# Layer one of a four-layer graph network: the destination's one-hot columns formed by ScalarE in two passes, for the next step, in place of VectorE's comparison

## The reference, cut to what matters

```python
src, dst = (edge_index[0], edge_index[1])
x = jnp.concatenate([node_features[src], node_features[dst], edge_features], axis=-1)
h = jax.nn.relu(x @ W1.T + b1)
messages = h @ W2.T + b2
agg = jax.ops.segment_sum(messages, dst, num_segments=node_features.shape[0])
# then a gated update of node_features by agg
```

## Time and profile before

| | us |
|---|---|
| median of 3 runs | 6944.7 |
| the profiled execution, its time | 6939.28 |
| its span, from first to last instruction | 6937.5 |
| TensorE busy | 5351.4 (77%) |
| GpSimd busy | 4647.9 (67%) |
| VectorE busy | 4547.1 (66%) |
| ScalarE busy | 2573.7 (37%) |

### The profile page before, as it was taken

How to read it: one execution, slowest core, us unless ns; L and a number is a source line. 1 busy time by engine, 2 the same in 40 slices (tenths; PEclk the granted TensorE clock), 3 DMA queues, 4 the chain that set the end, 5 groups by cost and what they waited for, 6 DMA issues and landing times. The chain is left out here.

```text
span 6937.5 us, 158305 instructions
## 1 busy us (share of the span) xinstructions
PE 5351.4 (77%) x35997; PEld 4099.9 (59%) x35998; DVE 4547.1 (66%) x7277; ACT 2573.7 (37%) x6699; POOL 4647.9 (67%) x4837
## 2 busy tenths in 40 slices
PE   5788888888888775667777777777786999669996
PEld 5678877777877654445555555555563444435554
DVE  9888888888888755588888888888853111231112
ACT  5355555555555443235454444444440000110000
POOL 5377777777777622277777777777736777457776
PEclk6566566666666655578888888888888999789998
DMA  9221222222222266334444444444419999489996
GB/s 398 78 54 54 54 53 55 55 55 55 53 55 55 59 213 201 85 116 141 140 145 136 144 140 137 143 141 140 140 57 263 329 328 329 102 245 318 317 318 174
DMA packets 913080, 1053.41 MB, mean 152 GB/s; under 512 B 329373, under 2 KB 758063, under 8 KB 910720
## 3 DMA queue, kind: packets, MB, share of 16 engines
q10 hardware_dynamic: 460709, 626.59, 27.6%
q1 hardware_dynamic: 303644, 264.09, 13.4%
q0 software_dynamic: 148624, 161.51, 8.8%
HBM read 692.23 MB, written 359.54 MB: 152 GB/s over the span
## 5 line engine op out<-in xcount | busy, mean ns | idle before, releaser
L945 POOL DMA_INDIRECT sorted_tab<-msg,row_at x1661 | 1606.3, 967 | 653.0 <-issue 490.0
L1530 POOL DMA_INDIRECT a_rows<-a_tab,idx x1661 | 1567.8, 944 | 535.3 <-issue 507.5
L2090 POOL DMA_INDIRECT h_rows<-h_tab,idx x1216 | 1155.4, 950 | 532.9 <-issue 355.0
L1824 ACT ACTIVATE adj<-ps_adj 128x392 bf16<-128x392 f32 x2080 | 943.9, 494 | 1038.5 <-PE ps_adj L1755 1032.1
L835 PE MATMUL ps_at<-next_at,lo_t 128*128 128x98 f32 x3328 | 1046.5, 411 | 324.6 <-ACT next_at L898 253.4
L835 PEld LDWEIGHTS ps_at<-next_at,lo_t 128*128 128x128 f32 x3328 | 771.3, 286 | 375.3 <-issue 194.7
L1755 PE MATMUL ps_adj<-one_key,one_lo 128*128 128x392 bf16 x2080 | 683.2, 366 | 381.4 <-ACT adj L1824 361.4
L1640 DVE TENSOR_TENSOR one_key<-ps_iota,key_all 128x1960 bf16<-128x1960 f32 x416 | 911.5, 2191 | 0.0
L2289 PE MATMUL ps_dense<-pieces,x_nm 128*128 128x480 bf16 x3332 | 725.6, 368 | 192.9 <-DVE low L2173 114.3
L863 PE MATMUL ps_msg<-u_win,hot_t 128*128 128x64 f32 x3328 | 840.7, 349 | 5.5 <-DVE hot_t L768 5.3
L863 PEld LDWEIGHTS ps_msg<-u_win,hot_t 128*128 128x128 f32 x3328 | 778.5, 287 | 9.6 <-DVE hot_t L768 9.0
(11 more groups left out here) (297 smaller groups left out, 8816.6 us busy)
## 6 DMA issues: line engine op xcount, KB each, us to landing
pieces<-adj_tab ACTq DMA_DIRECT2D x204, 1440.0 KB
adj_tab<-adj ACTq DMA_DIRECT2D x208, 980.0 KB
pieces<-adj_tab ACTq DMA_DIRECT2D x68, 1560.0 KB
sorted_tab<-acc_t SPq DMA_DIRECT2D x16, 4030.0 KB
landed_rows<-sorted_tab SPq DMA_DIRECT2D x124, 520.0 KB
lo_row<-lo_tab SPq DMA_DIRECT2D x209, 256.0 KB
ends_of<-edge_t SPq DMA_DIRECT2D x208, 132.0 KB
sorted_tab<-msg,row_at POOLq DMA_INDIRECT x1661
```

Source lines behind the costliest of these rows:

```text
L945: pool.indirect_dma_start(sorted_tab[:, :], bass.IndirectOffsetOnAxis(ap=row_at[:, r, k:k + 1], axis=0), msg[:, r, k, :], None).then_inc(s ...
L1530: pool.indirect_dma_start(dest[:, r, k, :], None, table[:, :], bass.IndirectOffsetOnAxis(ap=idx[:, r, k:k + 1], axis=0)).then_inc(landed[r ...
L1824: nc.scalar.activation(adj[:, b, :, k * WORD:(k + 1) * WORD], ps_adj[:, k % 2, 0:KEYS].rearrange("p (j d) -> p j d", d=WORD), ACT.Copy).th ...
L2090: pool.indirect_dma_start(rows_of[:, r, k, :], None, table[:, :], bass.IndirectOffsetOnAxis(ap=idx[:, r, k:k + 1], axis=0)).then_inc(lande ...
```

## The change

The comparison L1672 leaves VectorE, with its wait for the spread. ScalarE gets two instructions in its place, in a new function `ends_hot`: Square of `ps_dst` plus the negative number of the partition, and Relu of 1 minus that. Since all these numbers are whole, the result is 1 where they agree and 0 elsewhere. `ends_hot` for step s + 1 stands in ScalarE's round s, between the Relu of the messages and the copy of product 7; for step 0 it stands ahead of the loop. It waits for the spread of its step, and its second instruction for the first, on a semaphore of its own, `ends_squared`. The semaphore `hot_t_ready`, on which TensorE waits before the pre-activations, is now raised by ScalarE.

```diff
-                            need(dve, pre_done, s - 1)
-                            dve.wait_ge(dst_spread, s + 1)
-                            dve.tensor_scalar(ends_of[0:W, r, :, :], ps_dst[0:W, :, :], pidx[0:W, 0:1], None,
-                                              ALU.is_equal).then_inc(hot_t_ready, 1)
...
+                    def ends_hot(r, s):
+
+                        hold(act, pre_done, s - RING + 1)
+                        hold(act, dst_spread, s + 1)
+                        nc.scalar.activation(ends_of[0:W, r, :, :], ps_dst[0:W, :, :], ACT.Square,
+                                             bias=minus_pidx[0:W, 0:1]).then_inc(ends_squared, 1)
+                        hold(act, ends_squared, s + 1)
+                        nc.scalar.activation(ends_of[0:W, r, :, :], ends_of[0:W, r, :, :], ACT.Relu, bias=1.0,
+                                             scale=-1.0).then_inc(hot_t_ready, 1)
+
+                    ends_hot(0, 0)
                     for i in first_then_loop(act, TURNS):
                         for r in range(RING):
...
                             hold(act, pre_added, s + 1)
                             nc.scalar.activation(act_rows[:, b, :, 0:F], pre[:, b, :, :], ACT.Relu).then_inc(act_ready, 1)
+                            ends_hot((r + 1) % RING, s + 1)
                             if not first:
                                 keep(1 - b, s - 1, 2 * i + (r - 1) // 2, 7, GPS)
```

More of the change, by code:

```diff
@@ L1560, in gnn_kernel @@
             adj_out = [sem(f"l1_adj_out{b}") for b in range(2)]
-            counters, lo_hot, key_hot, adj_done, adj_kept = (
-                sem(f"l1_{n}") for n in ("counters", "lo_hot", "key_hot", "adj_done", "adj_kept"))
+            counters, lo_hot, key_hot, adj_done, adj_kept, ends_squared = (
+                sem(f"l1_{n}") for n in ("counters", "lo_hot", "key_hot", "adj_done", "adj_kept", "ends_squared"))
             iota_set, cleared, ones_ready, win_x, rel_f, rel_ready, dst_spread, hot_t_ready, hot_ready = (
```

## The result

| | us |
|---|---|
| predicted | 7400, range 7260 to 7540 |
| median of 3 runs after | 7713.72 (7708.45 to 7714.11) |
| median of 3 runs before | 6944.7 |
| ratio to before | 1.111, 95% interval 1.1091 to 1.1129 |

The change makes the kernel 769 us slower. The direction was forecast, the size was not: 769 us against 455 to 462, and the time lies outside the range. One of the 30 runs of the kernel before took 7860.7 us at a mean granted clock of 0.571 and is left out of every comparison; no trace read here is of that kind, for outside the stage each shows 4834 to 4847 us at a clock of about 0.74, and with that a mean of 0.571 can't come about.

A forecast was written before the change was run, and what follows sets the result against it. Bound: TensorE waiting for ScalarE's copies, not VectorE's busy share. Added 2.51 less 0.29 given back is 2.22 us a step, over 208 steps 462 us; on 6939.3 that gives 7401, rounded to 7400 us, range 7260 to 7540.

The forecast's parts named there:

- What bounds the kernel: Layer one's step of 10.13 us: TensorE waits for ScalarE's copies, and VectorE, though busiest, waits for TensorE's spread.
- What is taken away: VectorE's comparison, 1.28 us a step, and its wait for the spread; 60.5 us given back, 0.29 us a step.
- The part put down to the hot columns: TensorE's wait for VectorE's hot columns in layer one, 35.1 us, counted as given back in full, though doubted.
- What is added: Square 1.11 us and Relu 1.06 on ScalarE, with waits: 2.51 us between the messages' Relu and the copy of product 7.
- The place: Between the messages' Relu and copy 7: product 9 and TensorE's next round queue behind, so nearly all 2.51 us lengthens the step.
- What is late next: VectorE's wait for product 9 before expanding the low digits: ready 0.77 us ahead of TensorE, but 0.5 late at full clock.
- the floor: The new step's shortest time at any clock, 11.03 us, from VectorE's work through the new passes to product 9.
- The clock: In layer one's stage, granted clock averaging 0.85: a step was assumed to lose to the lower level about what it loses now.
- Rival (b): More waiting brings a second low-clock stretch, 1.08 us: 7513 us if every second step, 7626 if every step; chance 0.14.
- (a): The lower clock falls into TensorE's new wait at no cost; step 11.03 us, 7126 us in all; chance 0.11.
- (c): VectorE's 87% is the bound, ScalarE's idle half takes the passes, step falls to GpSimd's 10.0 us: 6888 us; chance 0.04.
- (d): No difference: TensorE's other waits absorb the new wait before the next sum by node, 6939 us; chance 0.02.

## Why the prediction was wrong

- **What bounds the kernel**: right. VectorE's share of busy time was no bound: with the comparison gone and the passes behind copy 9 the time stays within 0.2%, with seven eighths of it left out it falls by 19 us.
- **What is taken away**, 0.29 us a step: too much by two thirds. 19 us of 208 steps are 0.09 us. The part put down to the hot columns was doubted in the text and fell: in the kernel with one tile compared that wait is 142.4 us, not less than 35.1. The other part, 25.4 us for the addition, did go: only the wait at the stage's start is left. VectorE's busy time fell by 203 us in the changed kernel, not by 266.
- **What is added**: right, every term within 0.1 us. Square 1.11 us (1.11 forecast) and Relu 1.06 (1.06); Square starts 0.73 us after the spread's start (0.72), the hand-over between the two is 0.11 us (0.21). In all 2.43 against 2.51. The means of the trace are 1109 and 1056 ns:

```profile
L1836 ACT ACTIVATE ends_of<-ps_dst,minus_pidx 80x1024 f32<-80x1024 f32 x209 | 231.8, 1109 | 118.5 <-PE ps_dst L1718 104.0
L1839 ACT ACTIVATE ends_of<-ends_of 80x1024 f32<-80x1024 f32 x209 | 220.8, 1056 | 24.6
```

  The prediction sets the pair beside VectorE's one comparison and finds ScalarE slower. By the instruction it is not: each pass takes less than the comparison's 1.28 us, and the pair is longer because it is two. Its estimate of 3.84 us by a factor of three counts that factor once for two passes; the pair took 2.17 us.
- **The place**: right. Product 9 and the whole next round stood behind the passes, shown by the passes behind copy 9 (9 us lost), behind one copy (a fifth of the loss) and beside the kept comparison (all of it).
- **What is late next**: right. VectorE's new wait came, 874.7 us, and was covered: the addition waited for TensorE behind it. With sixteen idle products, at a clock of 0.97, it no longer did, and the step of 11.57 us came within 0.54 us of the floor.
- **The clock: this step failed.** It said that "a step loses to the lower level about what it loses now". The granted clock fell from 0.85 to 0.63, the time at the lower level rose from 3.0 to 10.2 us a step, and TensorE's own work grew from 7.50 to 9.43 us a step, where the sum had put that growth at nothing. With the clock put back to 0.85 the step is 12.33 us. The forecast of 12.35 for that clock was helped by luck: with 0.09 in place of 0.29 and 2.43 in place of 2.51 it would have been 12.47. So of the error of 1.50 us a step 1.4 us or more, some 290 us in all, is this term.
- **Rival (b)**, with 0.14, came nearest: more waiting did bring more of the lower level. But it did not come as a second stretch like the first. One stretch lasts through whole rounds, and the pre-activations and the products run in it too: the piece at 4024.9 above is at 0.50 and the pre-activations fill it. So its price for every step, 7626, which counts one more sum by node at the lower level, is 88 us short. Why the clock stays low so long is open.
- Rivals (a), (c) and (d) did not come. The range ended at 7540 because (b) was taken for every second step; a full (b) should have been in it, as nothing in the rows spoke against it, and even its 7626 falls short of 7714.

## What to carry to other kernels

Ask not which engine has room on average but what is queued behind the new instruction at its place: the same two passes cost 769 us between a Relu and a copy for which TensorE waits, and about nothing three copies later. A wait added to TensorE cost 1.79 us of idle time a step here and, where the granted clock already swung, 1.93 us of longer busy time. When such a swing shows in the rows, price that second sum too, and let the lower level hold for whole rounds in at least one rival. Where the clock is the loss, idle products in TensorE's own gaps are a cheap test. In one of the two kernels that had them in four gaps they also beat the kernel before, by 1%.

## What the runs showed of the hardware

The clock did not follow the length of the wait. With TensorE waiting longer in each round by the passes of 128, 512 and 1024 columns beside the kept comparison, the granted clock of the stage was 0.61, 0.59 and 0.66 (one run each), against 0.85 without them: the shortest passes brought the fall, and the longest had the highest clock of the three. By the Trainium skill, TensorE: Matmul & The Clock Gate, section Part 1: The HAM clock gate (the "warmup" mystery), the array's lower rate is the default and activity releases it. The runs agree so far as filling the wait with products raised the clock from 0.63 to 0.85 and 0.97, and adding 1656 products (eight in each of 207 rounds) shortened the kernel by 319 us.
